# Four of the sixteen absorbed weight couples moved from the preparation block into rounds 1, 3, 6 and 9 of the second attention

## The reference

```python
q_c = rmsnorm(hidden_states @ w_qa, g_qa)                 # 192 wide
q = (q_c @ w_qb).reshape(b, s, NH, QK)                    # 128 without position, 64 rotary
kv = hidden_states @ w_kva                                # 64 latent, 64 rotary
k_c = rmsnorm(k_c, g_kva)
kst = (k_c @ w_kvb).reshape(b, s, NH, ND + VD)            # keys and values of each head
scores = einsum('bhqd,bhkd->bhqk', query, key_s) * scaling
out = einsum('bhqk,bhkd->bhqd', softmax(scores), v)
return out.reshape(b, s, NH * VD) @ w_o
```

## Time and profile before

| what | value |
|---|---|
| runs | 903.23, 905.48, 910.38 us; median 905.48 |
| profiled execution | 904.65 us, its span 902.4 us, mean granted PE clock 0.961 |
| busy share of the span | PE 91%, DVE 76%, ACT 59%, POOL 60% |
| chain that ended last, by engine | PE 45%, DVE 8%, issue 5% |
| moved by DMA | 120.07 MB, 133 GB/s |

### The profile page before, as it was taken

One profiled execution on the slowest core, in us unless ns is written; L12 is line 12 of the kernel. 1 busy time (PEld: TensorE's weight loads), 2 busy tenths in 40 slices (PEclk: granted clock), 3 DMA queues, 4 the chain that ended last, 5 costly groups with the idle time before them and its releaser, 6 DMA issues.

```text
span 902.4 us, 15065 instructions
## 1 busy us (share of the span) xinstructions
PE 820.7 (91%) x4560; PEld 540.4 (60%) x4560; DVE 681.8 (76%) x1322; ACT 536.5 (59%) x1158; POOL 538.9 (60%) x481
## 2 busy tenths in 40 slices
PE   3899993699996996899999999999999999999997
PEld 1588873578784874465656565665655656564543
DVE  4768896644453467998989898889898899897662
ACT  5668874624233785666666666665666666665522
POOL 3334432012122236998889888887888989897213
PEclk8899997799998898999999999999999999999899
DMA  8530000845235441666666666665566766665511
GB/s 330 216 119 2 1 2 9 227 117 176 89 105 151 123 130 38 168 153 152 153 154 155 154 153 155 153 156 143 131 156 185 184 154 155 149 156 138 125 35 70
DMA packets 91460, 120.07 MB, mean 133 GB/s; under 512 B 30387, under 2 KB 41651, under 8 KB 91381
## 3 DMA queue, kind: packets, MB, share of 16 engines
q1 hardware_dynamic: 66804, 85.54, 34.3%
q10 hardware_dynamic: 24576, 33.59, 15.1%
HBM read 41.45 MB, written 2.10 MB: 48 GB/s over the span
## 4 chain that ended last, share of the span: by engine, by line
PE 45%; DVE 8%; issue 5%; ACTq 1%; ACT 1%; POOL 0%; DMA 0%; POOLq 0%; DVEq 0%; SPq 0%
PE bank L1536 11%; PE bank L1523 6%; PE bank L1524 4%; PE bank L1525 4%; PE bank L1550 4%; PE bank L1551 3%; PE bank L1552 3%; PE bank L1594 3%; DVE blk L1642 2%; DVE cT_lo L1714 2%; DVE stage_a L1178 2%; ACTq L1485 1%; DVE nmax L1626 1%; DVE stage_a L1181 1%; PE bank L1161 1%
## 5 line engine op out<-in xcount | busy, mean ns | idle before, releaser
L1626 DVE TENSOR_REDUCE nmax<-bank 128x1 f32<-128x512 f32 x256 | 174.1, 680 | 46.2 <-PE bank L1525 45.1
L1776 ACT ACTIVATE prob<-bank,nmax 128x512 f32<-128x512 f32 x172 | 118.3, 688 | 102.8 <-DVE nmax L1626 89.2
L1864 POOL TENSOR_TENSOR prob<-prob,rinv 128x512 f32<-128x512 f32 x129 | 132.6, 1043 | 33.4 <-DVE rinv L1634 32.0
L1523 PE MATMUL bank<-xk_hi,q_hi 128*128 128x512 f32 x256 | 113.2, 442 | 14.3 <-ACT prob L1776 8.5
L1642 DVE STREAM_TRANSPOSE blk<-prob 128x512 f32<-128x512 f32 x172 | 120.1, 698 | 6.3 <-ACT prob L1818 5.0
L1523 PEld LDWEIGHTS bank<-xk_hi,q_hi 128*128 128x128 f32 x256 | 48.5, 190 | 92.9 <-issue 53.0
L1524 PE MATMUL bank<-xk_lo,q_hi 128*128 128x512 f32 x256 | 102.0, 398 | 0.0
L1525 PE MATMUL bank<-xk_hi,q_lo 128*128 128x512 f32 x256 | 101.1, 395 | 0.0
L1195 POOL TENSOR_TENSOR q_lo<-stage_a,q_hi 128x512 fp32r<-128x512 f32 x64 | 82.2, 1285 | 25.1 <-ACT q_hi L1186 24.9
L1776 ACT ACTIVATE stage_a<-bank,nmax 128x512 f32<-128x512 f32 x84 | 57.8, 688 | 49.0 <-DVE nmax L1626 42.9
L1191 POOL TENSOR_TENSOR stage_a<-stage_a 128x512 f32<-128x512 f32 x64 | 82.9, 1295 | 4.8 <-DMA stage_a<-stage_a 4.8
(11 more groups left out here) (251 smaller groups left out, 1939.5 us busy)
## 6 DMA issues: line engine op xcount, KB each, us to landing
pT<-blk SPq DMA_DIRECT2D x256, 64.0 KB, 2.1
pT<-blk ACTq DMA_DIRECT2D x256, 64.0 KB, 2.1
raw_e<-blk SPq DMA_DIRECT2D x256, 64.0 KB, 2.1
raw_e<-blk ACTq DMA_DIRECT2D x256, 64.0 KB, 2.1
raw_e<-in_wo SPq DMA_DIRECT2D x16, 512.0 KB, 4.0
stage_a<-stage_a SPq DMA_DIRECT2D x128, 64.0 KB, 2.1
raw_e<-in_wmod SPq DMA_DIRECT2D x6, 1024.0 KB, 7.7
stage_a<-in_wmod SPq DMA_DIRECT2D x12, 512.0 KB, 4.4
```

The costliest lines, as they stand in the source:

```text
L1523: pe.matmul(sbk, q_hi[:, u % 2, q], xk_hi[:, 2, ks], start=True, stop=False)
L1626: dve.tensor_reduce(nmax[:, s % RING:s % RING + 1], s_bank[s % 2][:, :], AX.X, ALU.max, negate=True).then_inc(max_done, 1)
L1776: act.activation(prob[s % RING], s_bank[s % 2][:, :], ACT.Exp, bias=nmax[:, s % RING:s % RING + 1], accum_out=rsum[:, s % RING:s % RING + ...
L1864: pool.tensor_tensor(prob[s % RING], prob[s % RING], bc(rinv[:, s % RING:s % RING + 1], [P, S]), ALU.mult).then_inc(norm_pool, 1)
```

## The change

The preparation block makes couples 8 to 11 only (`PREP_COUPLES = 12`), and its SP list loads couples 10 to 13. In the last block couple 12 is made behind the scores of round 1, couple 13 in round 3, 14 in round 6 and 15 in round 9, in two banks (`ab_a`, `ab_b`) that the output projection uses later. ACT copies each result one round later, behind the exponential. SP loads couples 14 and 15 between the swaps of units 1 and 2. The moves of units 2 and 3, and the third tile of the first output projection, wait until all couples are made or copied.

```diff
+PREP_COUPLES = 12
...
-                        for j in range(FFN_COUPLES + 2, COUPLES // 2):
+                        for j in range(FFN_COUPLES + 2, PREP_COUPLES + 2):
                             load_couple(sp, j)
...
-                            if FFN_COUPLES + t < COUPLES // 2:
+                            if FFN_COUPLES + t < PREP_COUPLES:
                                 act_couple_a(act, FFN_COUPLES + t, a_ps)
                                 act_couple_b(act, FFN_COUPLES + t, b_ps)
...
-                            if FFN_COUPLES + t < COUPLES // 2:
+                            if FFN_COUPLES + t < PREP_COUPLES:
                                 pe_couple_a(pe, FFN_COUPLES + t, a_ps)
                                 pe_couple_b(pe, FFN_COUPLES + t, b_ps)
...
+            AB_AT = {1: 12, 3: 13, 6: 14, 9: 15}
+            ab_a, ab_b = o_bank[2][:, 0:2 * P], o_bank[3][:, :]
...
                 eng.wait_ge(blk_done, TPB * (u + 1))
+                if u in (2, 3):
+                    eng.wait_ge(ab_ps, COUPLES)
...
-                    for u in range(1, 4):
-                        swap(sp, u)
+                    swap(sp, 1)
+                    load_couple(sp, 14)
+                    load_couple(sp, 15)
+                    swap(sp, 2)
+                    swap(sp, 3)
...
+                            if j == 0 and n == 2:
+                                pe.wait_ge(ab_ev, COUPLES)
...
+                        if s in AB_AT:
+                            pe_couple_a(pe, AB_AT[s], ab_a)
+                            pe_couple_b(pe, AB_AT[s], ab_b)
...
+                        if s - 1 in AB_AT:
+                            act_couple_a(act, AB_AT[s - 1], ab_a)
+                            act_couple_b(act, AB_AT[s - 1], ab_b)
```

## The result

The changed kernel takes 913.03 us (median of 6 runs, 912.18 to 913.75). The kernel before took 907.13 us in the same sessions (6 runs, 903.23 to 910.38). The ratio is 1.0070 with an interval of 1.0046 to 1.0094: 6.3 us slower, from 4.2 to 8.5. The profiled execution took 912.69 us with a span of 910.5 us, against 904.65 and 902.4.

A forecast was written before the change was run, and what follows sets the result against it. The first rounds were held to be bound by a ring of swap (DMA), sum (POOL), rounding (ACT) and rotation (DVE), not PE's work. 904.65 - 1.4 + 7.45 = 910.7 us, stated as 911.0; forecast's own range 908.5 to 913.5, 8-in-10 range 904.5 to 917.0.

The forecast's parts named there:

- Preparation, forecast -1.4: Tiles 4 to 7 lose 7.8 us of PE; only 1.4 us, followed through ACT's queue, come off the path.
- rival (a): PE sets the preparation's pace and the rounds hide the couples: 7.8 us faster, 896.9 us; chance 0.04.
- Late swap, forecast sum +7.9 and exponential +7.7 us: Unit 2's swap, issued behind the loads, delays POOL's sum by 7.9 us and ACT's exponential of round 5 by 7.7.
- couple 13's start: In round 3, couple 13 waits for ACT's second copy of couple 12 and starts at 352.8 in the before-trace's times.
- The wait that I think decides: On SP, unit 2's swap stands behind couple 15's load, which waits for couple 13: POOL's sum +7.9 us.
- One of my own signs: Sign that the forecast is right: PE idle some 5 us between rounds 6 and 7.
- Couple 14 at 0: Couple 14, in round 6, lies within the wait for the late swap and costs 0.
- Couple 15 at +0.5: Couple 15, in round 9: 1.94 us of PE, about 1.4 covered by the exponential, leaving +0.5.
- given back: DVE's waits for a projection at 360.60 and the scores behind it vanish with PE ahead: -0.75 us.
- forecast 7.45: Lateness of the rounds from 10 on, kept to the end: 7.7 + 0.5 - 0.75 = 7.45 us.
- Rival (b): The late swap costs little; only the couples and half its delay stay: +2.6 us, 907 us; chance 0.18.
- Rival (c): PE falls to half clock in the preparation and rounds where it sits idle: adds 5.5 us, 916 us; chance 0.12.

The follow-up runs named there:

- the controls: Second profiles of the kernel before and the changed kernel, nothing edited: preparation 53.81 and 52.68 us, first rounds 29.41 and 38.85 us.
- e2: Kernel before, preparation without couples 12 to 15, nobody makes them, their last two loads left out: preparation 53.94 us, median 906.16 us, ratio 0.9991.
- e1: Changed kernel with SP reordered: swap 2 ahead of both loads, swap 3 ahead of load 15: first rounds 37.51 us, median 913.06 us, ratio 1.0061.
- e3: Kernel before with the swap of unit 2 held until the scores of round 6 are done: first rounds 33.89 us, median 912.43 us, ratio 1.0061.
- e8: Changed kernel with unread products where PE waits (12, 6 and 8): first rounds 37.72 us, median 915.05 us, ratio 1.0084.
- e5: Changed kernel with separate banks for even and odd couples and SP order swap 1, swap 2, load 14, swap 3, load 15: 910.39 us, ratio 1.0036.
- e12: Own banks; couples 8 to 10 in tiles 0 to 2, 11 and 12 in tiles 6 and 7, 13 to 15 in rounds 5, 9, 13: 903.11 us, 0.9978 against before.
- e4: Changed kernel with two more banks, so couples 13 and 15 have their own pair: first rounds 37.78 us, median 913.33 us, ratio 1.0074.

## Why the prediction was right or wrong

I had forecast 911.0 us, a shift of 6.05 us (910.7 less 904.65). The runs say 6.3. By the profile's stretches the change is +9.1 us (-0.65 and +9.8), +8.3 with the controls. The ends of the ratio's interval reach to 8.5; why the medians are some 2 us kinder than the stretches is not shown. What comes behind round 16 took 531.2 us in the profile before and 530.2 in the changed one, 528.9 and 529.5 in their second profiles, so that part alone moves by as much without any edit.

- **Preparation, forecast -1.4:** measured -0.65 and, in the control, -1.1. Right in kind: most of PE's 7.8 us lay beside ACT, as e2 shows, and rival (a) falls (53.94 us, where it wanted some 46). ACT's weights for `w_hi` started at 322.79 in place of 324.21, 1.42 us earlier where I had worked out 1.40. DVE's rotation behind them started at 329.97 in place of 331.08, only 1.1 earlier, since DVE lost 0.3 us beside POOL (last section). The last transpositions came 1.02 us earlier, and by their lowered clock another 0.36 was lost up to the first scores. In the second profile, without this, the gain is the 1.1.
- **Late swap, forecast sum +7.9 and exponential +7.7 us:** against the first scores the sum was 9.3 us late (19.43 us in place of 10.09) and the exponential of round 5 9.0 (363.24 - 341.46 in place of 354.93 - 342.12). The mechanism was there link by link; the size was off by 1.3 to 1.4 us, of which 0.4 is couple 13's start, 0.4 its slower second part (1.36 us from start to start in place of 1.01, as the clock fell: the scores behind it took 0.79), and 0.4 the swap's own last DMA (3.19 us in place of the 2.75 I had allowed).
- **"The wait that I think decides":** this is the step that failed. I held the late swap to be the cause; e1 removes it and gets 1.3 of 9.8 us back. Beside it lay a second delay of nearly the same length, couples 12 and 13 with the wait for the copy (6.3 us at round 7), and a third, couple 15 behind its load (8.4 at round 10 in e1). I had computed couple 13's start to within 0.4 us but used it only as the load's start, not as a delay of PE's own list. One of my own signs pointed there: PE was to be idle some 5 us between rounds 6 and 7, and was idle 2.60, because it came there late already.
- **Couple 14 at 0:** right in the changed kernel, since round 7 waited 2.60 us behind it anyway. **Couple 15 at +0.5 and "given back" -0.75:** from round 7 (9.0 us late) to round 16 (9.8) the rounds lost 0.8 more in place of gaining 0.25. Nothing of the given-back 0.75 is seen. These two and the 1.3 above make up the 2.3 us between the forecast 7.45 and 9.8.
- **Rival (b)**, half of the swap's delay hidden: true in part for the delay by itself (in e3 the swap was issued 6.8 us later against the first scores, 358.94 - 345.99 in place of 348.32 - 342.12, and cost 4.8, so that 2 of the 6.8 were hidden), not for the change as made. **Rival (c)**, 5.5 us by the clock: e8 shows the clock's fall and about 1.1 us of it in the rounds, and the preparation lost 0.4 of its gain to it, not all 1.4. The Trainium skill ("TensorE: Matmul & The Clock Gate", "Why this matters for your kernels") says that gaps between bursts bring half rate, and the trace agrees (granted clock 0.63 from 340 to 350 us); but here PE mostly waits for others in those rounds, so the rate costs little of the time. It costs more once a couple stands last in the chain: 1.9 us in e5.

The total came out near the forecast partly by luck: a preparation gain that was too large, rounds that were too small by 2.3 us, and medians that lie below the stretches.

## What to carry to other kernels

When several transfers and waits are made late by one edit, undo each alone and both together before naming a cause: of delays that lie side by side only the latest is seen, and removing it uncovers the next (1.3 us back for one, 1.1 for the other and 1.8 for both here, out of 9.8). Work for an idle engine is free only where its inputs have landed and its output space is clear: with the banks and the order of e5, the four couples cost 8.0 us in rounds 1, 3, 6 and 9, and 3.1 in rounds 1, 5, 9 and 13, where those of rounds 5 and 9 added nothing. A load that waits for late work belongs behind the short transfers that a ring needs, and it has to leave early enough for its own reader.

## What the runs showed of the hardware

**A DVE operation held by POOL.** The norm of a tile, 128 x 512 on DVE, takes 0.55 us when POOL is idle. In the changed kernel one took 1.33 us, while POOL's low part of the same size ran from 325.61 to 326.89. DVE's timeline, then POOL's:

```profile
325.85 1.33 DVE L174 TENSOR_SCALAR n_x<-x_res,mv,rstd 128x512 f32<-128x512 f32 x1
```

```profile
325.61 1.28 POOL L202 TENSOR_TENSOR n_h_lo<-n_f,n_h_hi 128x512 fp32r<-128x512 f32 x1 [0.82 <-ACT n_h_hi L198]
```

DVE ended 0.29 us after POOL. Before, the same norm took 0.86 us (325.63 to 326.49) beside a POOL operation of 324.94 to 326.21, and ended 0.28 us after it. Its duration is thus POOL's remaining time and a short rest. ACT's earlier start brought POOL's work onto DVE's. DVE went on to tile 5 without idle time at 327.10; ACT's root for it had started at 326.33, and before, DVE had followed such a root by 0.22 us, so it would have gone on at about 326.55. From ACT's weights to DVE's rotation it took 7.18 us in place of 6.87 in the end: 0.3 us of the preparation's gain went there. The Trainium skill ("SBUF — State Buffer", "SBUF: two separate sides") calls the port pair of the two engines an exclusive lock: whichever starts first has it, and the loser fully blocks. It says this of DVE operations in a two-port mode or with two inputs in SBUF; in which mode the norm ran no row shows. These rows agree in who waits. They do not show a full block, since the norm ends only 0.28 us after POOL though it needs 0.55 alone. e12 shows the other side: there DVE's norm started first and took 0.55 us, and POOL's low part, begun 0.26 us later, took 1.44 us in place of 1.27. DVE's timeline of e12, then POOL's:

```profile
324.72 0.55 DVE L174 TENSOR_SCALAR n_x<-x_res,mv,rstd 128x512 f32<-128x512 f32 x1
```

```profile
324.98 1.44 POOL L202 TENSOR_TENSOR n_h_lo<-n_f,n_h_hi 128x512 fp32r<-128x512 f32 x1 [1.43 <-ACT n_h_hi L198]
```

**A small DMA behind a large load lands later.** The swap lands 2.1 us after its issue, but its second half took 3.19 us behind a load of some 900 KB, 2.95 in the second profile and 3.45 in e4. I had allowed 2.75.
